# A graph attention's per-head shifts: their small arithmetic moves from VectorE to GpSimd, and the transpose of their parts to a later unit

## What is computed

```python
e = jax.nn.leaky_relu(as_n[src] + ad_n[dst], 0.2)      # one score per edge
m = jax.ops.segment_max(e, dst, num_segments=N)        # maximum per target
p = jnp.exp(e - m[dst])
s = jax.ops.segment_sum(p, dst, num_segments=N)
alpha = p / (s[dst] + 1e-16)
out = jax.ops.segment_sum(alpha[:, :, None] * h[src], dst, num_segments=N)
```

## Time and the profile before

| | |
|---|---|
| runs, median (lowest to highest) | 3988.24 us (3983.79 to 3988.59) |
| profiled execution, its own time | 3962.7 us |
| its span (first to last instruction) | 3961.1 us |
| busy over the span: PE, DVE, ACT, POOL | 92%, 50%, 42%, 39% |
| granted TensorE clock, mean | 0.969 of 2.4 GHz |
| att0, units | about 622 to 1106 us of the span |
| att2, units | about 1640 to 2060 us of the span |

### The profile page before, as it was taken

How to read it: one execution, slowest core, us unless ns; L and a number is a source line. 1 busy time by engine, 2 the same in 40 slices (tenths; PEclk the granted TensorE clock), 3 DMA queues, 4 the chain that set the end, 5 groups by cost and what they waited for, 6 DMA issues and landing times.

```text
span 3961.1 us, 58218 instructions
## 1 busy us (share of the span) xinstructions
PE 3625.3 (92%) x18463; PEld 2970.5 (75%) x18473; DVE 1961.6 (50%) x2783; ACT 1682.3 (42%) x2911; POOL 1556.8 (39%) x1168
## 2 busy tenths in 40 slices
PE   8998868999978897589989999999999999989998
PEld 4555437999978897333336999999999999955598
DVE  7245788888533635899955323333322231023334
ACT  1113677888832321499971333333333333300020
POOL 3887886666600001000001444444444444367500
PEclk9999998999989998799999999999999999999999
DMA  4343112232233302311024555555555553379801
GB/s 147 98 112 74 45 23 62 78 90 78 71 114 100 119 20 82 115 40 40 33 73 138 186 183 187 186 183 175 175 183 185 188 183 112 102 274 305 247 9 63
DMA packets 176460, 483.10 MB, mean 122 GB/s; under 512 B 40798, under 2 KB 57205, under 8 KB 176342
## 3 DMA queue, kind: packets, MB, share of 16 engines
q1 hardware_dynamic: 87414, 201.95, 15.7%
q0 software_dynamic: 54368, 185.24, 15.3%
q10 hardware_dynamic: 34560, 94.45, 6.7%
HBM read 357.64 MB, written 123.55 MB: 121 GB/s over the span
## 4 chain that ended last, share of the span: by engine, by line
PE 40%; ACT 7%; POOL 5%; issue 3%; DVE 2%; DMA 1%; SPq 0%; DVEq 0%; ACTq 0%; POOLq 0%
PE ps L1893 30%; POOL work L1975 5%; ACT work L1279 3%; PE ps L1881 3%; ACT ps L1270 3%; PE ps L1558 3%; PE ps L306 2%; PE ps L298 1%; DVE work L1101 1%; PE ps L1216 1%; DVE work L1129 0%; DMA work<-msg_d,work 0%; ACT work L1289 0%; DMA ct<-x_d 0%; PE ps L324 0%
## 5 line engine op out<-in xcount | busy, mean ns | idle before, releaser
L1893 PE MATMUL ps<-wsplit,xsplit 128*128 x6840 | 1236.9, 337 | 2.7 <-DVEq L1833 2.7
L1893 PEld LDWEIGHTS ps<-wsplit,xsplit 128*128 128x128 f32 x6840 | 1181.5, 188 | 2.9 <-issue 2.9
L1830 DVE CAST wsplit<-wplain 128x768 fp32r<-128x768 f32 x204 | 117.1, 574 | 759.6 <-PE ps L1893 744.3
L1860 POOL TENSOR_TENSOR xsplit<-ct,xsplit 128x768 fp32r<-128x768 f32 x190 | 369.9, 1947 | 296.6 <-ACTq L1925 296.6
L1279 ACT ACTIVATE work<-ps,work 128x418 f32<-128x418 f32 x720 | 437.7, 631 | 107.7 <-PE ps L1189 102.3
L1930 ACT ACTIVATE ct<-ps,invs 128x768 f32<-128x768 f32 x190 | 171.4, 902 | 713.1 <-PE ps L1893 713.1
L1226 PE MATMUL ps<-hbuf,work 128*128 128x193 f32 x2400 | 455.2, 328 | 15.4 <-DVE work L1143 13.1
L1226 PEld LDWEIGHTS ps<-hbuf,work 128*128 128x128 f32 x2400 | 407.4, 190 | 43.4 <-issue 16.9
L1270 ACT ACTIVATE ps<-work,lr 128x418 f32<-128x418 f32 x720 | 431.4, 633 | 6.0 <-DMA work<-lrow_d 6.0
L1129 DVE SCALAR_TENSOR_TENSOR work<-work,cnt 128x1250 f32<-128x1250 f32 x240 | 349.9, 1458 | 133.3 <-ACT work L1279 132.7
L1855 POOL DMA_INDIRECT ct<-x_d,relrec x190 | 200.5, 1055 | 455.9 <-PE ps L1881 448.3
(11 more groups left out here) (212 smaller groups left out, 4399.8 us busy)
## 6 DMA issues: line engine op xcount, KB each, us to landing
wplain<-in_L_gnn_W_rel SPq DMA_DIRECT2D x34, 2304.0 KB, 9.7
msg_d<-ct ACTq DMA_DIRECT2D x190, 384.0 KB, 2.6
work<-lrow_d SPq DMA_DIRECT2D x47, 625.0 KB, 3.7
feat_d<-work ACTq DMA_DIRECT2D x30, 386.0 KB, 4.3
hbuf<-feat_d SPq DMA_DIRECT2D x60, 193.0 KB, 2.5
gat_d<-work POOLq DMA_DIRECT2D x12, 960.0 KB, 5.2
xplain<-gat_d SPq DMA_DIRECT2D x30, 384.0 KB, 3.2
work<-xa_d SPq DMA_DIRECT2D x27, 384.0 KB, 3.5
```

The lines of the kernel that those rows point to most:

```text
L1860: g.tensor_tensor(xlo7[:, k % XW, :], xt7[:, k % 2].rearrange("p c n -> p (c n)"), xhi7[:, k % XW, :].bitcast(F32), ALU.subtract).then_inc ...
L1893: last = pe.matmul(ps[:, 4 + 2 * (u % 2) + h, 0:HALF], x[:, u, c * P:(c + 1) * P], w[:, bass.ds(base + (c * D + h * HALF), HALF)], start=( ...
```

## The change

`shifts` is now written for any engine. It has 10 instructions of 128 x 10 (12 in att2) in place of 7 (9), as the two three-operand forms are spelled out. DVE still runs it for heads 0 and 1. From head 2 on POOL runs it, as soon as the head's ten maxima are there and the parts of the head before have been turned. DVE keeps the turn alone, in the fifth unit (10h + 4) of the head before, behind a wait for the parts. On SP `shift` moves forward by one head in the list, with that: in the turn of the loop for head h stands `shift(h + 1)` where `shift(h + 2)` stood, at its end, behind the features.

```diff
@@ sp @@
                         for k in range(5):
                             unit_done(NT * h + 2 + k)
                             features(h + 2, 2 * k, 2 * k + 2)
-                    if h + 2 < H:
-                        shift(h + 2)
+                    if 2 <= h + 1 < H:
+                        shift(h + 1)
+            def shifts(self, eng, step, h):
+                m, r0 = self.mh[h % 2], self.columns[h][1]
+                if self.isolated:
+                    step(eng.tensor_scalar(self.y, m, 0.1 * NONE, -NONE, ALU.is_lt, ALU.mult))
+                    step(eng.tensor_tensor(m, m, self.y, ALU.add))
+                step(eng.tensor_tensor(self.z, m, lr[:, r0:r0 + NT], ALU.add))
+                step(eng.tensor_scalar(self.M, self.z, 0.0, 1.0 - SLOPE, ALU.max, ALU.mult))
+                step(eng.tensor_scalar(self.c, self.z, SLOPE, None, ALU.mult))
+                step(eng.tensor_tensor(self.M, self.M, self.c, ALU.add))
+                step(eng.tensor_scalar(self.M, self.M, -1.25, None, ALU.mult))
+                step(eng.tensor_tensor(self.c, self.M, self.r4[:, r0:r0 + NT], ALU.add))
+                b = [self.parts[:, k * NT:(k + 1) * NT] for k in range(3)]
+                step(eng.tensor_copy(b[0], self.c))
+                step(eng.tensor_tensor(self.d, self.c, b[0], ALU.subtract))
+                step(eng.tensor_copy(b[1], self.d))
+                step(eng.tensor_tensor(b[2], self.d, b[1], ALU.subtract))
+            def pool_shifts(self, g, step, h):
+                if h >= self.H:
+                    return
+                g.wait_ge(self.s_max, self.at["max"] + NT * (h + 1))
+                g.wait_ge(self.s_c, self.at["c"] + h)
+                self.shifts(g, step, h)
+                g.sem_inc(s_parts, 1)
+            def pool_narrow(self, g, step):
+                for h in range(self.H):
+                    self.pool_shifts(g, step, h + 2)
@@ dve, maximum @@
-                    if j == NT - 1:
-                        shifts(h)
-                def shifts(h):
-...
-                    step(v.scalar_tensor_tensor(self.M, self.z, SLOPE, self.z, ALU.mult, ALU.max))
-                    step(v.scalar_tensor_tensor(self.c, self.M, -1.25, self.r4[:, r0:r0 + NT], ALU.mult, ALU.add))
+                    if j == NT - 1 and h < 2:
+                        v.wait_ge(self.s_max, self.at["max"] + NT * (h + 1))
+                        self.shifts(v, step, h)
+                        turn(h)
+                def turn(h):
                     if h >= 2:
+                        v.wait_ge(s_parts, self.at["parts"] + h - 1)
                         v.wait_ge(self.s_c_out, self.at["c_out"] + 64 * (h - 1))
                     v.transpose(self.turned[h % 2], self.parts).then_inc(self.s_c, 1)
@@ dve, the loop over units @@
+                    if q % NT == 4 and 2 <= q // NT + 1 < H:
+                        turn(q // NT + 1)
```

More of the change, by code:

```diff
@@ L946, in sp_lr_rows @@
             sp.wait_ge(att_sems[0][2], 16 * n)
+        s_parts = sem("att_parts_ready")
         att_sems = ([sem(f"att_{n}") for n in ("columns_turned", "columns_copied", "rows_stored")],
@@ L1003, in __init__ @@
                 self.at = {"l_row": 8 * H, "r_row": 8 * H, "shift_row": 8 * H, "stored": 8 * H, "cols": 1, "max": T, "c": H, "c_out": 64 * H,
-                           "relu": 3 * T, "add": 3 * T, "exp": 3 * T, "p": T, "agg": T, "free": 5 * H, "out": H}
+                           "relu": 3 * T, "add": 3 * T, "exp": 3 * T, "p": T, "agg": T, "free": 5 * H, "out": H, "parts": H - 2}
                 if not self.narrow:
@@ L1070, in sp, with pool @@
                             features(h + 2, 2 * k, 2 * k + 2)
-                    if h + 2 < H:
-                        shift(h + 2)
-            def pool(self, g, beside=lambda h: None):
+                    if 2 <= h + 1 < H:
[26 more added lines that the diff above has]
+                    self.pool_shifts(g, step, h + 2)
+            def pool(self, g, step, beside=lambda h: None):
                 C = self.C
@@ L2133, in _ @@
             g.wait_ge(s_invd, 16)
-            att0.pool(g, lambda h: gather_inverses(g, 16 * h, min(RT, 16 * (h + 1))))
+            att0.pool(g, step, lambda h: gather_inverses(g, 16 * h, min(RT, 16 * (h + 1))))
             g.wait_ge(s_invs, 16 * RT)
@@ L2140, in _ @@
             meet(g)
+            att2.pool_narrow(g, step)
             pool_root(g, step)
```

11 lines of the change are left out of this document (removed).

## The result

The changed kernel takes **3998.64 us** in the median of 8 runs (3996.8 to 4000.9), the kernel before 3988.23 us (8 runs, 3983.79 to 3988.86). The ratio is 1.0029, 95% interval 1.0019 to 1.0038: slower by 10.4 us. The prediction said 3995 us.

The account below looks back on a forecast made before the run. The prediction took PE to set the pace in att0 and ACT to be busy nearly throughout att2, with DVE having time to spare. Its terms, 2.4 + 3.8 + 0.5 = 6.7 us, added to 3988.24 gave 3995 us, range 3987 to 4004.

Parts of the forecast that it names:

- DVE is not on the path: At each head's end: the 1.57 us of `shifts` in att0 leave an engine with time to spare, so no gain.
- The rival that the wait was an artefact of modelled ends: At `evict`: DVE's time was on the path after all, so the kernel gets faster, 3980 us; chance 0.05.
- Part 1: Heads 0 and 1 of both attentions: three more small DVE instructions each, 0.6 us paid four times, 2.4 us.
- Part 2: SP's list in att0: PE waits for `crow` behind the features, 0.42 us in each of heads 2 to 10, 3.8 us.
- a rival for all heads: Att0: stores held behind the features by 1.39 us more, PE waiting 1.66 us nine times, 4006 us; chance 0.18.
- the forecast case: Att0: PE waits 0.15 to 0.8 us a head for `crow`, total time 3992 to 3999 us; chance 0.50.
- the third rival: Att0: the stores are held behind the features on SP's queue, 4006 us; chance 0.18.
- Part 3: POOL's arithmetic: 0.45 us a step, more when meeting long DVE instructions; costs DVE 0.05 us a head, 0.5 us.
- Part 4: The turn on DVE in the fifth unit: moved without a price; up to 0.2 us a head could show in att2.
- The sum: Whole kernel: 2.4 + 3.8 + 0.5 = 6.7 us slower.

Follow-up runs that it names:

- the kernel with both edits: The changed kernel with shifts behind the fourth features transfer on SP and the two-instruction short form for heads 0 and 1: 3989.88 us, ratio 1.0003.
- The experiment with more on DVE: The kernel before, with the last four instructions of the shifts done three times on DVE for heads 2 to 11: 4035.98 us, ratio 1.0118.
- the kernel with the late turn: The kernel before, arithmetic kept on DVE, only the turn moved five units later, with the changed kernel's list on SP: 3996.34 us, ratio 1.0016.

## Why the prediction was right, and where it was off

**DVE is not on the path**: right. 1.57 us were taken away at each head's end, and no head got shorter. In the kernel with both edits, where PE is not late, `evict` waits 0.96 us for PE where it waited 0.36, and PE's 1.2 us stay. The experiment with more on DVE shows how near it was: of 1.65 us more, all but about the first 0.4 us were lost. The rival that the wait was an artefact of modelled ends is out.

**Part 1, heads 0 and 1**: right, and too small, 3.3 us for 2.4. In the second attention it is 0.59 and 0.66 where I had 0.6 each. In the first it is 1.22 and 0.83: the term took every small instruction at 0.20 us, and single ones that GpSimd's indirect transfers catch take 0.36 to 0.57.

**Part 2, SP's list**: the mechanism is right, the wait is where it was said to be, and it is in the nine heads that were named. The size is 6.3 us for 3.8. For seven heads the 0.42 us were nearly right: they are 0.43 to 0.58 us longer, 0.50 in the mean. In the head of the rows the steps of the sum were short by 0.05 us between the last features and the first store, 0.16 us in the stores and 0.03 us behind the load, where 0.15 us had been added for all of it. The other two are 1.36 and 1.41 us longer, since there the way from store to load takes 3.71 us, near the 4.05 of the earlier trace rows. I had that as a rival for all heads and as 0.15 us for the forecast; it is two heads in nine. And the 4.05 us of the earlier trace rows were not a price of standing behind features: there are none in that attention, and that store too has an instruction packet beside it. Moving the shifts up one place gives it all back, and moving them alone costs it. That the forecast case held to 3999 us, and the measurement is 3998.64, is partly luck: its 0.15 to 0.8 us a head do not cover the two slow ones.

The Trainium skill (DMA: Bandwidth & Descriptors, section Queues, rings and completion order) says that an SP queue's descriptors are taken in order on each engine. The trace agrees at the start of the stores: their first data packet begins 1.40 us behind the first store's issue where it was 0.83 us before, and the features' 256 packets begin from 899.66 to 900.83 us, across it. At the end little is left of it: the last one begins 2.41 us behind the issue for 2.30, and seven of the nine loads go out 0.1 to 0.25 us later after the first store than before. (Where the prediction names the third rival here, it is the second of its list.)

**Part 3, GpSimd's arithmetic**: I charged 0.5 us for the heads of the second attention. The first profile showed just that, 0.05 us a head, and it would have been easy to call it confirmed. Four other kernels with the same arithmetic have 32.40 to 32.42 us and a fifth 32.42 to 32.44, and of those without it two have 32.42 to 32.44 and three 32.40 or 32.41. The term is nothing that the runs can tell from zero. A step's price was put too high: 0.45 us, of which 0.3 between two instructions as between two gathers. It is 0.19 to 0.30 us with 0.08 between:

```profile
909.76 0.21 POOL L1090 TENSOR_TENSOR work<-work 128x10 f32<-128x10 f32 x1
910.03 0.19 POOL L1091 CAST work<-work 128x10 bf16<-128x10 f32 x1
```

That one meets a long DVE instruction and waits for its end was right. In the second attention (POOL):

```profile
1807.40 0.28 POOL L1080 TENSOR_SCALAR work<-work 128x10 f32<-128x10 f32 x1 [23.39 <-DVE work L1136]
1807.76 1.32 POOL L1081 TENSOR_TENSOR work<-work 128x10 f32<-128x10 f32 x1
1809.16 1.30 POOL L1082 TENSOR_TENSOR work<-work,lr 128x10 f32<-128x10 f32 x1
...
1815.11 1.36 POOL L1092 TENSOR_TENSOR work<-work 128x10 bf16<-128x10 f32 x1
```

Five of the twelve met one where I had eight, and all took 9.1 us for 12.6. In the first attention it was 5.1 us for 7.5. The Trainium skill (GPSIMD Engine Reference, section Key points) warns of this contention; the trace agrees as far as GpSimd goes, which takes five to seven times as long for such a step. DVE's long instructions don't show it: `weigh` takes 1.46 us in the mean of the second attention with the arithmetic on GpSimd and without. Its small ones do, beside GpSimd's indirect transfers, by the rows above.

**Part 4, the turn**: nothing, as said. No head in the kernel with the late turn shows it.

**The sum**: 6.3 + 3.3 = 9.6 us. 0.4 us more comes at the start of the second attention, where one of DVE's ten maxima starts 0.57 us behind the end of the one before it and not 0.17. All eight profiles with arithmetic on GpSimd have it, and the six without don't; why, no run tells. That makes 10.0 of the 10.4 us. The forecast had 6.7: its first term came out 0.9 us larger, its second 2.5 us, its third at nothing for 0.5, and the 0.4 us were in none. The two profiles also differ by 1.9 us in front of the first attention, where the changed kernel is ahead, and by 1.7 us between the two attentions, where it is behind; that these cancel in the 10.3 us is luck.

## What to carry to other kernels

Work taken off an engine is worth what the wait behind it says, and nothing of what its busy time says. The wait gives the reserve in both directions: here 0.36 us at one point of a head of 39.42, and 1.65 us put there cost 1.2.

When a small transfer is moved behind others on a queue, subtract its latest start from the moment when it is wanted, for every head. The margin was 0.3 us short, for two heads more than 1 us, and one place earlier on the list was enough. An engine with spare time takes over work up to its own idle time per round, however late the result may come: GpSimd had 2.7 us of it in a head, not the 15.3 us until the turn.

## What the hardware showed that I had not expected

A GpSimd instruction on 128 x 10 elements takes 0.19 to 0.30 us with 0.08 us to the next, close to DVE's 0.17 and 0.20 from start to start. Caught by a DVE instruction of 1.46 us it takes 1.22 to 1.37 us in the changed kernel, and ends some 0.06 us behind it.

Four stores of 1.9 KB right behind a load of 193 KB are 0.1 to 0.25 us slower in seven heads and 1.05 us slower in two, and these two are the same heads in all four profiles with that list (0.90 to 1.39 us slower). In all eight an instruction packet of 8 or 16 KB lies among them, in none of the 28 others.

A CAST or TENSOR_SCALAR of 128 x 10 on DVE can take up to 0.57 us for 0.17, and then it ends with the instruction of an indirect transfer on GpSimd, 20 times out of 20.

ScalarE stood still for up to 3.9, 7.6 and 2.2 us at a time in three kernels, with nothing in the trace that it waited for on its core (in the first of them the DMA engines' share was 0.01 from 1045 to 1060 us), and there TensorE's granted clock fell from 1.00 to 0.50 for some 8 us behind it; the cause is open.
